# Loading the rows of the last body between the combination's first two hands and its next two

## What is computed

```
x  = x + L0_attn(ln(x)) * silu(L0_ffn(ln(x)))
xn = ln(x)
s  = L1_attn(xn)
probs = softmax(xn @ wg.T); w, idx = top_k(probs, 2); w = w / sum(w)
y_e = (silu(xn @ w1[e].T) * (xn @ w3[e].T)) @ w2[e].T          (for each expert e)
out = x + s * silu(sum over the two chosen e of w_e * y_e)
```

## Time and profile before

| | |
|---|---|
| Median of 3 runs | 791.23 us (790.57 to 791.6) |
| The profiled execution's own time | 792.25 us |
| Its span (first to last instruction) | 790.5 us |
| Mean granted TensorE clock | 0.910 |
| Busy share of the span | PE 81%, DVE 72%, ACT 62%, POOL 42% |
| Expert phase, first transposed tile to end of span | 609.8 to 790.5 us |

### The profile page before, as it was taken

The page is one execution under the profiler, slowest core; times in us unless marked ns, Lnnn a source line. Parts: engine busy times, 40 slices in busy tenths (PEclk is TensorE's granted clock), DMA queues, the critical chain, the costliest instruction groups (busy, mean ns, idle before and its releaser), DMA issues. The chain is left out here.

```text
span 790.5 us, 15056 instructions
## 1 busy us (share of the span) xinstructions
PE 640.4 (81%) x4547; PEld 350.3 (44%) x4548; DVE 566.0 (72%) x1455; ACT 492.6 (62%) x860; POOL 334.5 (42%) x490
## 2 busy tenths in 40 slices
PE   4576667999999999999999868877444998999760
PEld 3455452333333333333333467765433555566430
DVE  3999996888888979797977757845434545556487
ACT  2287866999999999999999724334122434444452
POOL 0244443444444444444444330537271465555361
PEclk9799987999999999999999977969575999999895
DMA  7000000005555555555550050112011222222615
GB/s 190 15 27 27 15 29 25 1 2 101 100 100 100 100 100 100 100 100 100 100 100 4 1 186 1 55 55 73 21 51 33 61 68 70 71 73 67 186 58 159
DMA packets 76263, 55.83 MB, mean 71 GB/s; under 512 B 6528, under 2 KB 70848, under 8 KB 75968
## 3 DMA queue, kind: packets, MB, share of 16 engines
q1 hardware_dynamic: 70688, 45.84, 27.1%
q0 software_dynamic: 4352, 8.95, 3.4%
q10 hardware_dynamic: 1184, 0.56, 0.3%
HBM read 15.32 MB, written 28.48 MB: 55 GB/s over the span
## 5 line engine op out<-in xcount | busy, mean ns | idle before, releaser
L784 ACT ACTIVATE attend_prob<-attend_ring 128x1024 f32<-128x1024 f32 (+1 forms) x320 | 280.4, 954 | 16.8 <-PE attend_ring L930 14.9
L728 POOL TENSOR_SCALAR_AFFINE_SELECT attend_prob<-attend_prob 128x256 f32<-128x256 f32 x256 | 118.3, 485 | 142.2 <-ACT attend_prob L784 141.2
L950 PE MATMUL attend_ps_o<-attend_prob,attend_v_slot 128*32 128x512 f32 (+3 forms) x1536 | 157.4, 498 | 0.0
L1771 POOL DMA_INDIRECT expert_outputs<-expert_y_out,expert_goal_now x72 | 71.9, 998 | 70.0 <-DVE expert_y_out L1816 36.8
L930 PE MATMUL attend_ring<-attend_qk_slot 32*128 32x512 f16 (+3 forms) x672 | 80.1, 329 | 8.2 <-ACT attend_prob L784 6.3
L1024 POOL DMA_INDIRECT slots<-rows,slot_index x64 | 62.6, 978 | 46.7 <-DVE linear_norm_sum L1225 27.7
L1938 PE MATMUL expert_ps_h<-w,expert_x_t 128*128 x144 | 81.6, 649 | 0.8 <-ACT expert_x_t L1874 0.8
L1895 ACT ACTIVATE expert_tanh<-expert_ps_h 128x256 f32<-128x256 f32 x72 | 27.7, 385 | 74.9 <-PE expert_ps_h L1938 51.4
L930 PEld LDWEIGHTS attend_ring<-attend_qk_slot 32*128 32x128 f16 x672 | 22.4, 91 | 106.8 <-ACT attend_prob L784 37.6
L1800 DVE SCALAR_TENSOR_TENSOR expert_silu<-expert_tanh,expert_ps_h 128x256 f32<-128x256 f32 x72 | 30.3, 421 | 53.2 <-ACT expert_tanh L1895 33.5
L1960 PE MATMUL expert_ps_y<-w,expert_hidden_t 128*128 x288 | 48.9, 294 | 6.2 <-DVE expert_y_out L1816 3.7
(11 more groups left out here) (280 smaller groups left out, 1289.7 us busy)
## 6 DMA issues: line engine op xcount, KB each, us to landing
slots<-attend_zeros SPq DMA_DIRECT2D x24, 709.5 KB, 10.1
attend_qk_slot<-qk_parts SPq DMA_DIRECT2D x14, 512.0 KB, 3.1
x_pairs<-slots SPq DMA_DIRECT2D x72, 64.5 KB
expert_y_in<-expert_outputs SPq DMA_DIRECT2D x8, 512.0 KB, 6.2
xn_all<-project_xn SPq DMA_DIRECT2D x8, 256.0 KB, 2.3
w<-w_laid SPq DMA_DIRECT2D x1, 2048.0 KB, 7.7
rows<-rows SPq DMA_DIRECT2D x4, 512.0 KB
out<-expert_result SPq DMA_DIRECT2D x8, 256.0 KB, 3.1
```

The costliest lines, as they stand in the source:

```text
L728: ins = nc.gpsimd.affine_select(out=edge, in_=edge, compare_op=ALU.is_ge, fill=0.0, base=0, pattern=[[0, 2], [1, P]], channel_multiplier=-1)
L784: nc.scalar.activation(probs(k, pair)[:, :, 0:width], scores[:, :, 0:width], ACT.Exp, scale=HD ** -0.5).then_inc(exp_made[u][pair], 1)
L950: ins = nc.tensor.matmul(ps_o[RB * s:RB * (s + 1), off:QC], v4[slot][:, j, s], probs(k, s // 2)[:, s % 2, at:at + cols], start=j == 0, sto ...
L1771: pool.indirect_dma_start(m.outputs, bass.IndirectOffsetOnAxis(goal_now[i][:, j:j + 1], 0), y_out[i][:, j * P:(j + 1) * P], None).then_inc ...
```

## The change

In SP's program at the end of the expert phase, the loads of hands 2 and 3 move behind `load_next(10)`, the only iteration of that loop. Nothing else changes; the numbers of DMAs and their sizes stay as they are.

```
             for i in range(2):
                 sp.wait_ge(y_sent[i], 16 * TRIO * ((-(-SEEN // TRIO) + 1 - i) // 2))
-            for k in range(LINE):
-                load_y(k)
+            load_y(0), load_y(1)
             for b in range(OLD + 1, BODIES - 1):
                 load_next(b)
+            load_y(2), load_y(3)
             load_y(4), load_y(5)
```

## The result

The changed kernel took 788.77 us as the median of 14 runs (787.21 to 791.24); the kernel before, in 14 runs beside it, 792.42 us (789.41 to 794.38). The ratio is 0.9958, with a 95% interval of 0.9946 to 0.9970: faster by 0.42%, between 2.4 and 4.3 us. The forecast had the direction and, in the main, the mechanism. Its 786.6 us lies 2.2 us too low, 788.77 us lies just outside its range, which ended at 788.7, and its gain of 4.65 us lies above the interval's end.

What follows compares the result with a forecast made beforehand. The prediction took PE's wait for body 11's rows, queued behind four hands, as the bound. It summed 3.85 us of stall + 1.0 of clock - 0.2 for hand 2 = 4.65 us, so 791.23 became 786.6 us, range 785.7 to 788.7.

Steps and rivals of the forecast that it cites:

- What bounded the kernel: Before tile 66's transpose, PE idles 4.49 us for body 11's rows, queued behind hands 0 to 3.
- SP's new order and the rows' landing: On SP's queue: first trio issued from 736.1 us, hand 2 at 742.7; tile 66's rows land at 741.1.
- What the tile sets going: After tile 66, on ACT and DVE: weighted_sum(1) at 745.3 us, 4.85 us earlier.
- PE's later start: At tile 66: the stall's share of the gain, 744.96 - 741.1 = 3.85 us.
- The clock: Behind tile 66's stall: PE's granted clock no longer falls, worth 1.0 us.
- Hand 2: At weigh(2) on ACT: hand 2 is late and takes 0.2 us off the gain.
- Hand 2's landing: Before weigh(2): lands 4.2 us after issue, at 746.9 us, 0.2 us late; possibly 0.9 us late behind the second trio.
- the level: Whole kernel: starting median 791.23 us; the range allowed 0.5 us for the spread of runs.
- the combination takes part back: Rival: weighted_sum(0) on DVE, 1.13 us, pushes the tiles' work; gain 3.5 us, time 787.8 us; chance 0.15.
- the change does nothing: Rival: row loads wait for something else, or the queue serves them last; 791.2 us; chance 0.06.
- The late hand: Rival: hand 2 comes too late at weigh(2) on ACT, kernel slower at 792.9 us; chance 0.04.
- The larger gain: Rival: tile 66's rows at 740.9 us and hand 2 on time; gain 5.0 us, time 786.2 us; chance 0.05.

Runs made afterwards that it cites:

- swap_2_3: The changed kernel with hand 3 issued ahead of hand 2: ratio 0.9968 to the kernel before.
- hands_between: The changed kernel with hands 2 and 3 issued between body 11's two trios of row loads: ratios 0.9935 and 0.9941 to the kernel before.
- before_again: The kernel before, run again with no edit: ratio 0.9999 to itself.
- three_ahead: The changed kernel with hand 2 also moved ahead of body 11's row loads, hand 3 behind them: ratio 0.9967 to the kernel before.
- awake_before: The kernel before with 16 identity multiplications on PE filling the stall ahead of tile 66's transpose, loads unchanged: ratio 0.9980 to the kernel before.
- after_again: The changed kernel, run again with no edit: ratio 0.9945 to the kernel before.

## Why the prediction was right in its steps and wrong in its time

**What bounded the kernel: right, with the weight elsewhere.** The rows of body 11 came behind four hands, as the distances at two, three and four hands show. The prediction told it by the queue; 3.15 of the 3.64 us were SP's later issue, which its walk of SP's order had nevertheless in it.

**SP's new order and the rows' landing: right.** Measured from tile 65, and so put on the old trace's time by taking off 2.27 us, the trio's third load was issued at 738.8 (predicted 738.5 to 738.9), tile 66 was transposed at 741.3 (741.1), hand 2 was issued at 742.55 (742.7). Only the first of the trio's loads was later than forecast, 739.11 - 2.27 = 736.8 against 736.1.

**What the tile sets going: right.** weighted_sum(1) at 747.53 - 2.27 = 745.26 against 745.3.

**The size of the gain: nearly right.** Of 4.65 us predicted, 4.43 us showed in the pair of traces and 4.5 us in the means. The terms: PE's later start, predicted 3.85 us, measured 6.37 - 2.72 = 3.65 us between the means. The clock, predicted 1.0 us, measured 1.1 us with the stall filled. Hand 2, predicted -0.2 us, measured -0.44 us. The sum of the measured terms is 4.3 us, within 0.2 us of the 4.5 us seen.

**Hand 2's landing: too early.** It landed after 4.92 us and not after the 4.2 us of the earlier trace rows, at 749.74 - 2.27 = 747.5 against 746.9. That is the case which the prediction named and did not take, hand 2 0.9 us late with the second trio still in front of it. ACT idled 1.25 to 1.35 us before weigh(2) in three traces and not a few tenths, and idling over 1 us there was one of the prediction's own signs of being wrong; it cost 0.44 us.

The estimate of 3.2 us for a hand by the Trainium skill (DMA: Bandwidth & Descriptors, on the anatomy of one DMA), whose figures were fitted for POOL's kind of DMA, is further off still on SP's queue: 4.92 us here, and 4.2 us in the earlier trace rows.

**The step that failed: the level, the 791.23 in "791.23 - 4.65", and the "0.5 us of spread" in the range.** I put the shift on a median of three runs that lay within 1.0 us of each other, and took 0.5 us as the spread. Fourteen runs of the same kernel spread over 5.0 us (789.41 to 794.38) with a median of 792.42, 1.2 us higher. The forecast gain on that level gives 787.8 us, and the range moved up by 1.2 us would have held 788.77. The traces show that there is variation ahead of the change: tile 65 stood 2.27 us apart in two kernels whose PE programs are the same up to there.

**The other 1.0 us: the gain of 4.65.** The medians of the first comparison differ by 3.65 us, its interval ends at 4.3 us. The later ratios, 0.9945 and 0.9943, are 4.1 and 4.5 us; my estimate from the three comparisons, weighted by their intervals, is 3.9 us, give or take 0.6. The traces say 4.5 us at the third-last copy, and from tile 65 to the end of the span 51.87 us before (two traces) against 47.53 us after (three), 4.3 us. The difference between the two is the clock in the last two tiles: it fell there in one of three traces of the changed kernel (last copy 3.46 us behind the third-last instead of 2.95) and in none of two of the kernel before. Traces are too few to say that the change brings it about. The 4.3 us of the traces and the 3.9 us of the runs agree within the interval; that the first comparison came out lower still stays open, and may be chance.

**The rivals.** That the combination takes part back fell, though not for want of contact: weighted_sum(0) ran from 743.57 without a gap behind a copy and held the next activation, whose tanh was done at 742.87 + 0.39 = 743.26, until 744.62, but DVE idled 0.85 us before the activation of (10, 5) at 746.54, so it was made up there. That the change does nothing fell. The late hand was the right place; its first 1.3 us of waiting cost 0.44 us, and only what swap_2_3 added to that went one for one. It did not cost the gain. The larger gain, 5.0 us, did not come here, but hands_between, which has hand 2 on time, shows it in its traces: 25.56 - 20.61 = 4.95 us at the third-last copy.

## What to carry to other kernels

The loads of SP's queue landed here in the order of issue, and the issue itself took SP's time, up to 2.00 us for one load. So put each load where its due time puts it, read both its issue and its landing, and price a move on both sides: here a hand of 512 KB ahead of a load cost that load 1.6 to 2.0 us, and the hand that was moved back cost 0.44 us for the first 1.3 us of ACT's waiting and one for one beyond. A stall of TensorE can cost more than its length by the clock that falls behind it, here 1.1 us. Compare two traces from the last instruction that the change cannot touch, and take the level and the spread of the time from more runs than three.

## What the runs showed of the hardware

The clock: after 4.5 us without work on PE the granted clock was 0.55 over the next 6 us, and 0.58 in before_again after 4.64 us; after 2.93 us in three_ahead and 1.05 us in awake_before it was 1.00. In four traces of the eleven (after_again, three_ahead, hands_between, awake_before) the last one or two down-multiplications took up to 1.22 us instead of 0.71 us, with pauses of under 1 us in front of them; the first trace of hands_between shows a granted clock of 0.81 from 716 to 726 us, in which PE works up to 724.74:

```profile
716.00:726.00 10.00, 6.69 (x30) 4.00 (x29) 6.57 (x19) 4.88 (x15) 5.91 (x7) 0.81 0.11 35
```

The chips: the kernel before took 753.14 us on one chip, and 794.49 and 795.51 us in two sets on another; the record does not say on which chip the first comparison's 792.42 us were taken. In the traces tile 0 of the expert phase was transposed at 579.8 and at 609.8 us, and the linear phase ahead of it took that difference (its first statistics, line 1172, stand at 467.5 and 466.2 us). From tile 0 to tile 65 it was 121.0 and 128.9 us, and from tile 65 on the two agree to 0.2 us. Three waits of 13 to 14 us stand in the slower trace between 400 and 610 us; in the faster one the first of them is 5.8 us long and the other two are missing (first number: us in total, then times, then the longest):

```profile
POOL expert_spare_row L1778 <- POOLq L104: 14.4, 1, 14.4
ACT linear_xn_turned L1455 <- DMA norm_in<-L_attn_norm_const: 14.2, 1, 14.2
...
DVE linear_kv_masked L1242 <- remote: 13.2, 1, 13.2
```

What holds these engines there was not tested.
